# Four places in place of two for the copied gate and up columns of the experts, each copied one block sooner

## The chip, the cores and the metric

The kernel runs on one core of a Trainium2 chip. The metric is the device time of one execution in microseconds (us), lower is better; what is compared is the median of several runs. The profile is one further execution, recorded by the hardware profiler, and has a time of its own.

## The reference, cut to what matters

The input x has 4 sequences of 1024 tokens with 256 channels. It is normalised, and two things are added to it: a windowed self-attention, and a mixture of experts with one shared expert and 64 routed ones, of which each token uses eight. The change touches the routed experts alone:

```python
gate_out = jnp.einsum('bsh,ehi->bsei', hidden_states, expert_gate_k)
up_out = jnp.einsum('bsh,ehi->bsei', hidden_states, expert_up_k)
expert_act = jax.nn.silu(gate_out) * up_out
routed = jnp.einsum('bsei,eih->bsh', expert_act * router_mask[..., None], expert_down_k)
```

All of it is float32. An expert's weights are a 256 x 128 gate, a 256 x 128 up and a 128 x 256 down matrix.

## The kernel before

The program runs five stages one after the other: `project` (normalisation, q, k, v, router), `route` (sorting the 32768 pairs of token and expert into 320 blocks of 128 slots, one expert to a block; also the shared expert), `experts`, `attend` and `merge`. Semaphores are set and awaited by hand. The change is in `experts` alone, about 270 to 883 us of the profile.

**A block** (r) goes through this chain. GpSimd gathers its 128 token rows from DRAM into one of 16 places of `xb` (L903), once the result of block r-16 has been taken. TensorE transposes them into PSUM (L923, `turn_x`), ScalarE copies that to `xTe` (L970, `copy_x`), and TensorE forms gate and up, in this order, from `xTe` and the weights in `wgu` (L934, `gate_up`). ScalarE applies silu to the gate (L978), VectorE multiplies by up (L1021), TensorE multiplies by the down matrix (L944, `down`), VectorE scales the result by the token's weight into one of four places of `ys` (L1030, `take_y`), and SyncE stores it (L869). A place of `ys` is written again when the store of four blocks before has landed.

**Weights.** An expert's three matrices come by one DMA into one of eight places of `wb`. SyncE issues it in step r for block r+8, behind the store of block r (L479); it moves bytes only where block r+8 is the first of its expert. ScalarE copies the 512 gate and up columns from `wb` to `wgu` (L986, `copy_w`) for every block; the down matrix is read from `wb` directly.

**Order of the work.** All engines run their own instructions in the order written. A loop turn has 16 blocks; the first and last turn stand outside the loop, 18 are in it. In step r TensorE does `down(r)`, `turn_x(r+3)`, `gate_up(r+2)`; ScalarE does `copy_x(r+3)`, `silu(r+2)`, `copy_w(r+3)`; VectorE does the product of r+1, then `take_y(r)`; SyncE stores r and issues the weights of r+8. `wgu` has NW = 2 places, so `copy_w(r)` waits until the up product of block r-2 is done, besides the landing of its weights. `gate_up(r)` waits for `wgu_ready`, for `xTe` and for the product of block r-2, whose PSUM banks it takes over. The last four loop turns (blocks 256 to 319) also load the first stacks of q and k for `attend`, one DMA at every fourth block.

Of the kernel before, what the change touches and what calls it, by code (L numbers as in the profile page):

```python
# [67 lines left out]
WCOLS = 2 * 2 * I + D  # L68
XR = 16
WR = 8  # L70
# [413 lines left out]
def fields(engine, table, n, at, most):  # L484


    regs = [engine.alloc_register(f"entry_{next(NUMBER)}") for k in range(n)]
    engine.load(regs, table[0:1, bass.ds(at, n)])
    return [bass.RuntimeValue.of_register_unchecked(reg, min_val=0, max_val=most) for reg in regs]


def unpack(words, k, most):


    word = words[k // PACK]
    return ((word >> (PACK_BITS * (k % PACK))) & ((1 << PACK_BITS) - 1)).with_bounds(min_val=0, max_val=most)
# [310 lines left out]
def experts(nc, ctx, keep, w_exp):  # L807
# [9 lines left out]
    def sb(name, shape, dt=F32):  # L817
        return ctx.enter_context(nc.sbuf_tensor(name, shape, dt))
# [4 lines left out]
    def sems(name, n):  # L823
        return [sem(f"{name}{i}") for i in range(n)]

    NW = 2

# [5 lines left out]
    aT = sb("aT", [P, 2, P])  # L835
    wgu = sb("wgu", [P, NW, 2, 2 * I])

# [12 lines left out]
    def first(i):  # L850
        return isinstance(i, int) and i == 0

    def exists(i, r):
        return not isinstance(i, int) or i * XR + r < NB_ROUTED

    def every(engine, step):

        step(0)
        with engine.Fori(1, LAST) as i:
            step(i)  # L860
        step(LAST)

    with nc.Block() as block:
        @block.sync
        def _(sp):
            def store(i, r):

                sp.wait_ge(ys_ready, i * XR + r + 1)
                sp.dma_start(y_d[bass.ds(i * (XR * P) + r * P, P), :], ys[:, r % YR, :]).then_inc(y_out[r % YR], 16)  # L869

            def step(i, stacks=None):


                for r in range(XR):
                    if stacks is not None and r % 4 == 2:
                        load_stack(sp, keep, stacks[0], stacks[0], stacks[1], r // 4)
                    if r % 8 == 0:
                        load = fields(sp, meta[:, LOAD_F, :], 8, i * XR + (r + WR), (WR << PLACE_BIT) - 1)
                    store(i, r)
                    if exists(i, r + WR):  # L880
                        sp.wait_ge(y_ready, i * XR + (r + 1))
                        load_weights(sp, keep, w_exp, r, load[r % 8])

            step(0)
            with sp.Fori(1, LAST - 3) as i:
                step(i)
            for k in range(4):
                step(LAST - 3 + k, (k // 2, k % 2))
# [27 lines left out]
        def _(pe):  # L916
# [10 lines left out]
            def gate_up(i, r):  # L927
# [4 lines left out]
                for part, bank, ready in ((0, G, g_ready), (1, U, u_ready)):  # L932
                    for h in range(2):
                        last = nc.tensor.matmul(banks[bank + r % 2][:, 0:P],  # L934
                                                wgu[:, r % NW, h, part * I:(part + 1) * I], xT[:, r % 2, h, :],
                                                start=(h == 0), stop=(h == 1))
# [26 lines left out]
        @block.scalar  # L963
        def _(act):
            def copy_x(i, r):

                if not first(i) or r > 1:
                    act.wait_ge(u_ready, i * XR + (r - 1))
                act.wait_ge(px_ready, i * XR + r + 1)
                nc.scalar.copy(xT[:, r % 2, :, :].rearrange("p h q -> p (h q)"), banks[PX + r % 2][:, 0:D]  # L970
                               ).then_inc(xT_ready, 1)

            def silu(i, r):

                if not first(i) or r > 1:
                    act.wait_ge(act_ready, i * XR + (r - 1))
                act.wait_ge(g_ready, i * XR + r + 1)
                nc.scalar.activation(gate[:, r % 2, :], banks[G + r % 2][:, 0:P], ACT.Silu).then_inc(gate_ready, 1)  # L978

            def copy_w(i, r, at):  # L980


                act.wait_ge(w_in[r % WR], i * (16 * XR // WR) + 16 * (r // WR + 1))
                if not first(i) or r >= NW:
                    act.wait_ge(u_ready, i * XR + (r - NW + 1))
                nc.scalar.copy(wgu[:, r % NW, :, :].rearrange("p h c -> p (h c)"), wb[:, bass.ds(at, 4 * I)]  # L986
                        ).then_inc(wgu_ready, 1)

            def step(i):
                words = fields(act, packed[:, AT_F, :], XR // PACK + 1, i * (XR // PACK), WORD)  # L990
                at = [unpack(words, k, WR - 1) * WCOLS for k in range(XR + 3)]
                for r in range(XR):
                    if exists(i, r + 3):
                        copy_x(i, r + 3)
                    if exists(i, r + 2):
                        silu(i, r + 2)
                    if exists(i, r + 3):
                        copy_w(i, r + 3, at[r + 3])

            words = fields(act, packed[:, AT_F, :], 1, 0, WORD)  # L1000
            at = [unpack(words, k, WR - 1) * WCOLS for k in range(3)]
            copy_w(0, 0, at[0])
            copy_w(0, 1, at[1])
            copy_x(0, 0)
            copy_x(0, 1)
            silu(0, 0)
            copy_w(0, 2, at[2])
            copy_x(0, 2)
            silu(0, 1)
            every(act, step)  # L1010

        @block.vector
# [593 lines left out]
def build(nc, x, w_qk, w_vr, w_proj, w_exp, c_f32, out):  # L1606
    with ExitStack() as ctx:
# [44 lines left out]
        with ExitStack() as inner:  # L1652
            experts(nc, inner, keep, w_exp)
# [56 lines left out]
```

## Time and profile before

| | |
|---|---|
| median of 3 runs | 1404.14 us (1404.03 to 1408.12) |
| the profiled execution's own time | 1411.81 us |
| its span in the trace | 1410.0 us |
| granted TensorE clock, mean over the span | 0.946 of full speed |
| busy, share of the span | TensorE 88%, weight loads of TensorE 58%, VectorE 58%, ScalarE 56%, GpSimd 46% |

In rows of the profile PE is TensorE's matmuls, PEld its loads of the stationary operand, DVE VectorE, ACT ScalarE, POOL GpSimd, and SPq the DMA instructions of SyncE. A float32 matmul stands there as two instructions. A bracket at the end of a row gives how long the engine was idle before it and what ended that; "issue" is time in which it waited for nothing that the profile shows.

### The profile page before, as it was taken

How to read it: one execution, taken by the hardware profiler on the slowest of the kernel's cores; microseconds unless marked ns; L12 is line 12 of the kernel's file. 1: busy time of each engine (PE TensorE's matmuls, PEld its weight loads, DVE VectorE, ACT ScalarE, POOL GpSimd, SP SyncE). 2: the span in 40 equal slices, each digit the busy share in tenths (PEclk: the TensorE clock that was granted, in tenths of full speed). 3: DMA queues.
4: the chain of work that ended last, by engine and by line, in shares of the span. 5: the costliest groups of instructions: out<-in, count | busy, mean ns of one | idle time of the engine just before them, and what ended most of it. 6: DMA issues, size and time to landing. Idle time of an engine off the chain costs nothing. (4 is left out here: it accounts for less than half of the span.)

```text
span 1410.0 us, 37368 instructions
## 1 busy us (share of the span) xinstructions
PE 1241.7 (88%) x8360; PEld 824.5 (58%) x8361; DVE 824.4 (58%) x2576; ACT 785.9 (56%) x1900; POOL 644.4 (46%) x666
## 2 busy tenths in 40 slices
PE   6777699679999999998999889888888888888879
PEld 3444366568888788887888768233334333344337
DVE  5778588524444344443444334878777777777733
ACT  3444345446777677775777656255555554555553
POOL 1333303255555455554555443555555555555520
PEclk9999899889999999999999999799989999889989
DMA  7677600167777677775777897255544545444413
GB/s 249 182 185 189 171 1 23 41 170 209 213 215 211 195 218 213 210 220 177 217 210 230 199 163 145 76 131 126 143 116 116 129 125 130 124 114 116 119 46 120
DMA packets 150486, 218.01 MB, mean 155 GB/s; under 512 B 22817, under 2 KB 123169, under 8 KB 150434
## 3 DMA queue, kind: packets, MB, share of 16 engines
q1 hardware_dynamic: 121954, 130.59, 31.7%
q0 software_dynamic: 27648, 86.02, 25.1%
q10 hardware_dynamic: 832, 0.79, 0.2%
q8 instruction: 23, 0.38, 0.1%
q14 instruction: 29, 0.24, 0.1%
HBM read 247.46 MB, written 70.26 MB: 225 GB/s over the span
## 5 line engine op out<-in xcount | busy, mean ns | idle before, releaser
L903 POOL DMA_INDIRECT xb<-token_rows,idx_ring_x x320 | 304.0, 950 | 280.3 <-issue 180.3
L934 PE MATMUL psum<-xTe,wgu 128*128 128x128 f32 x2560 | 372.8, 289 | 23.4 <-ACT wgu L986 22.2
L934 PEld LDWEIGHTS psum<-xTe,wgu 128*128 128x128 f32 x2560 | 314.5, 193 | 82.2 <-ACT wgu L986 60.3
L1521 POOL DMA_INDIRECT yg<-expert_rows,idx_ring x256 | 260.4, 1017 | 209.9 <-PE psum L1229 130.0
L1351 ACT ACTIVATE pT<-psum 128x384 f32<-128x384 f32 (+1 forms) x512 | 218.3, 465 | 227.8 <-PE psum L1229 198.0
L1416 DVE CUSTOM_DVE_ANT_0 masked<-psum,mask_q 128x384 f32<-128x384 f32 (+1 forms) x512 | 252.9, 520 | 89.4 <-PE psum L1236 48.5
L1030 DVE TENSOR_SCALAR ys<-psum,xb 128x256 f32<-128x256 f32 x320 | 154.9, 484 | 155.8 <-PE psum L944 113.6
L1021 DVE TENSOR_TENSOR aT<-gate,psum 128x128 f32<-128x128 f32 x320 | 91.9, 287 | 213.6 <-PE psum L934 169.6
L1236 PE MATMUL psum<-qk 96*128 96x384 bf16 (+1 forms) x512 | 176.5, 347 | 40.9 <-DVE nmax L1416 32.4
L986 ACT COPY wgu<-wb 128x512 f32 x320 | 198.5, 620 | 12.3 <-PEq L544 4.4
L944 PE MATMUL psum<-wb,aT 128*128 x640 | 195.6, 388 | 9.7 <-DVE aT L1021 6.8
L1244 PE MATMUL psum<-qk 98*128 98x384 bf16 (+1 forms) x512 | 173.9, 341 | 12.7 <-ACT pT L1351 10.6
L970 ACT COPY xTe<-psum 128x256 f32<-128x256 f32 x320 | 119.4, 373 | 82.8 <-PE psum L923 32.9
L978 ACT ACTIVATE gate<-psum 128x128 f32<-128x128 f32 x320 | 89.0, 278 | 119.5 <-issue 77.3
L1229 PE MATMUL psum<-consts_bf 128*128 128x256 bf16 (+1 forms) x512 | 142.5, 279 | 0.0
L1257 PE MATMUL psum<-pT,va 128*32 128x256 f32 (+1 forms) x1792 | 129.7, 363 | 0.2 <-ACT pT L1351 0.2
L923 PE MATMUL psum<-ident,xb 128*128 128x128 f32 x640 | 123.8, 276 | 6.7 <-DMA xb<-token_rows,idx_ring_x 6.7
L1236 PEld LDWEIGHTS psum<-qk 96*128 96x128 bf16 x512 | 53.3, 104 | 105.1 <-DVE nmax L1416 58.6
L923 PEld LDWEIGHTS psum<-ident,xb 128*128 128x128 f32 x640 | 90.8, 142 | 40.0 <-DMA xb<-token_rows,idx_ring_x 7.5
L944 PEld LDWEIGHTS psum<-wb,aT 128*128 128x128 f32 x640 | 98.1, 194 | 14.4 <-issue 14.1
L1244 PEld LDWEIGHTS psum<-qk 98*128 98x128 bf16 x512 | 51.8, 101 | 92.8 <-issue 44.3
L1454 DVE TENSOR_TENSOR yg<-yg 128x512 f32<-128x512 f32 (+1 forms) x128 | 79.7, 624 | 0.1
(139 smaller groups left out, 1175.2 us busy)
## 6 DMA issues: line engine op xcount, KB each, us to landing
wb<-in_w_exp SPq DMA_DIRECT2D x320, 384.0 KB
expert_rows<-ys SPq DMA_DIRECT2D x320, 128.0 KB
qk<-q_stacks SPq DMA_DIRECT2D x32, 384.0 KB
q_stacks<-wb SPq DMA_DIRECT2D x32, 192.0 KB, 2.7
qk<-k_parts SPq DMA_DIRECT2D x32, 192.0 KB
k_parts<-wb SPq DMA_DIRECT2D x28, 192.0 KB, 2.7
token_rows<-rows SPq DMA_DIRECT2D x8, 640.0 KB, 3.3
xb<-token_rows,idx_ring_x POOLq DMA_INDIRECT x320
```

The costliest lines, as they stand in the source:

```text
L903: nc.gpsimd.indirect_dma_start(out=xb[:, r, :], out_offset=None, in_=rows_d, in_offset=bass.IndirectOffsetOnAxis(ap=idx_ring[:, q, r:r + 1 ...
L923: last = nc.tensor.transpose(banks[PX + r % 2][:, h * P:(h + 1) * P], xb[:, r % XR, h * P:(h + 1) * P], ident[:, :])
L934: last = nc.tensor.matmul(banks[bank + r % 2][:, 0:P], wgu[:, r % NW, h, part * I:(part + 1) * I], xT[:, r % 2, h, :], start=(h == 0), sto ...
L944: nc.tensor.matmul(banks[Y + r % 2][:, 0:D], aT[:, r % 2, :], wb[:, bass.ds(at + 4 * I, D)], start=True, stop=True).then_inc(y_ready, 1)
L986: nc.scalar.copy(wgu[:, r % NW, :, :].rearrange("p h c -> p (h c)"), wb[:, bass.ds(at, 4 * I)]).then_inc(wgu_ready, 1)
L1030: nc.vector.tensor_scalar(ys[:, r % YR, :], banks[Y + r % 2][:, 0:D], xb[:, r % XR, bass.ds(e + W_COL, 1)], None, ALU.mult).then_inc(ys_re ...
L1229: return nc.tensor.matmul(out, ident_b, mask, start=False, stop=True, skip_group_check=True)
L1236: nc.tensor.matmul(ring_bank(ahead_entry(like(g), i, hh))[:, 0:(hi - lo) * P], qk[0:KS, q, 0, hh, i * P:(i + 1) * P], qk[0:KS, q, 1, hh, l ...
L1244: nc.tensor.matmul(key_bank(j, hh)[:, 0:(hi - lo) * P], qk[0:KM, q, 1, hh, j * P:(j + 1) * P], qk[0:KM, q, 0, hh, lo * P:hi * P], start=Tr ...
L1351: nc.scalar.activation(pT[:, (j % 2) * HG + hh, 0:(hi - lo) * P], key_bank(j, hh)[:, 0:(hi - lo) * P], ACT.Exp).then_inc(p_ready, 1)
L1416: nc.vector.tensor_tensor_reduce(masked[:, (i * HG + hh) % 2, 0:(hi - lo) * P], ring_bank(place)[:, 0:(hi - lo) * P], mask_q[:, side:side ...
L1521: nc.gpsimd.indirect_dma_start(out=yg[:, h, k, :], out_offset=None, in_=y_d, in_offset=bass.IndirectOffsetOnAxis(ap=idx_ring[:, h, k:k + 1 ...
```

## The change

`wgu` gets four places, and ScalarE copies the columns of block r+4 in step r, where it copied those of block r+3. The copy of a fourth block is added ahead of the first turn. Each copy then waits for the up product of block r-4 in place of r-2. The number of copies is the same, and TensorE's order is the same.

```diff
-    NW = 2
+    NW = 4
...
-                at = [unpack(words, k, WR - 1) * WCOLS for k in range(XR + 3)]
+                at = [unpack(words, k, WR - 1) * WCOLS for k in range(XR + NW)]
                 for r in range(XR):
                     if exists(i, r + 3):
                         copy_x(i, r + 3)
                     if exists(i, r + 2):
                         silu(i, r + 2)
-                    if exists(i, r + 3):
-                        copy_w(i, r + 3, at[r + 3])
+                    if exists(i, r + NW):
+                        copy_w(i, r + NW, at[r + NW])
...
-            at = [unpack(words, k, WR - 1) * WCOLS for k in range(3)]
+            at = [unpack(words, k, WR - 1) * WCOLS for k in range(NW)]
...
             silu(0, 1)
+            copy_w(0, 3, at[3])
             every(act, step)
```

## Rows read from the trace of the kernel before

**Rows 1.** The page: engines over the span, and the groups of lines 934 and 986.
```profile
PE 1241.7 (88%) x8360; PEld 824.5 (58%) x8361; DVE 824.4 (58%) x2576; ACT 785.9 (56%) x1900; POOL 644.4 (46%) x666
L934 PEld LDWEIGHTS psum<-xTe,wgu 128*128 128x128 f32 x2560 | 314.5, 193 | 82.2 <-ACT wgu L986 60.3
L986 ACT COPY wgu<-wb 128x512 f32 x320 | 198.5, 620 | 12.3 <-PEq L544 4.4
```

**Rows 2.** Windows: length, PE, PEld, DVE, ACT, POOL busy, PE clock, DMA share, GB/s.
```profile
322.00:761.00 439.00, 428.22 (x2885) 356.15 (x2886) 185.61 (x482) 302.56 (x722) 231.44 (x257) 1.00 0.71 210
761.00:799.00 38.00, 34.91 (x237) 28.95 (x236) 14.79 (x40) 24.51 (x60) 18.51 (x22) 1.00 0.75 207
799.00:865.00 66.00, 58.81 (x396) 48.90 (x395) 23.85 (x65) 40.42 (x100) 34.47 (x31) 1.00 1.01 175
```

**Rows 3.** Timeline of one block's step: start, duration, engine, line, operation.
```profile
503.02 0.97 PEld L934 LDWEIGHTS psum<-xTe,wgu 128*128 128x128 f32 x8 [0.21 <-ACT wgu L986]
...
503.21 0.48 DVE L1030 TENSOR_SCALAR ys<-psum,xb 128x256 f32<-128x256 f32 x1 [0.42 <-PE psum L944]
503.83 0.28 ACT L978 ACTIVATE gate<-psum 128x128 f32<-128x128 f32 x1 [0.37 <-issue]
504.13 0.62 ACT L986 COPY wgu<-wb 128x512 f32 x1
504.28 0.29 DVE L1021 TENSOR_TENSOR aT<-gate,psum 128x128 f32<-128x128 f32 x1 [0.58 <-PE psum L934]
504.80 0.97 PEld L934 LDWEIGHTS psum<-xTe,wgu 128*128 128x128 f32 x8 [0.20 <-ACT wgu L986]
504.87 0.37 ACT L970 COPY xTe<-psum 128x256 f32<-128x256 f32 x1
505.61 0.28 ACT L978 ACTIVATE gate<-psum 128x128 f32<-128x128 f32 x1 [0.36 <-issue]
```

**Rows 4.** Timeline of the weight loads of TensorE across the end of a loop turn.
```profile
524.37 0.97 PEld L934 LDWEIGHTS psum<-xTe,wgu 128*128 128x128 f32 x8 [0.20 <-ACT wgu L986]
525.67 0.30 PEld L944 LDWEIGHTS psum<-wb,aT 128*128 128x128 f32 x2 [0.33 <-issue]
525.99 0.36 PEld L923 LDWEIGHTS psum<-ident,xb 128*128 128x128 f32 x2
526.32 0.97 PEld L934 LDWEIGHTS psum<-xTe,wgu 128*128 128x128 f32 x8
527.21 0.30 PEld L944 LDWEIGHTS psum<-wb,aT 128*128 128x128 f32 x2
```

**Rows 5.** Timeline: the results of blocks 16, 256, 276, 308 and 319 being taken.
```profile
322.18 0.48 DVE L1030 TENSOR_SCALAR ys<-psum,xb 128x256 f32<-128x256 f32 x1
760.66 0.48 DVE L1030 TENSOR_SCALAR ys<-psum,xb 128x256 f32<-128x256 f32 x1 [0.68 <-PE psum L944]
799.25 0.48 DVE L1030 TENSOR_SCALAR ys<-psum,xb 128x256 f32<-128x256 f32 x1 [0.35 <-PE psum L944]
865.00 0.48 DVE L1030 TENSOR_SCALAR ys<-psum,xb 128x256 f32<-128x256 f32 x1 [0.85 <-DMA expert_rows<-ys]
882.47 0.48 DVE L1030 TENSOR_SCALAR ys<-psum,xb 128x256 f32<-128x256 f32 x1 [0.61 <-PE psum L944]
```

**Rows 6.** Timeline of SyncE's DMA instructions and the gathers between them.
```profile
504.22 0.35 SPq L869 DMA_DIRECT2D expert_rows<-ys  x1
504.50 0.95 POOL L903 DMA_INDIRECT xb<-token_rows,idx_ring_x  x1 [0.77 <-issue]
505.14 0.67 SPq L479 DMA_DIRECT2D wb<-in_w_exp  x1
505.91 0.35 SPq L869 DMA_DIRECT2D expert_rows<-ys  x1
```

**Rows 7.** Timeline and windows: one load that moves bytes, and the traffic after it.
```profile
508.63 0.30 SPq L479 DMA_DIRECT2D wb<-in_w_exp  x1
510.00:512.00 2.00, 1.96 (x15) 1.48 (x13) 0.77 (x2) 1.37 (x5) 1.17 (x2) 1.00 0.94 311
```

## The prediction, made before the changed kernel was run

> **What bounds the kernel now.** I read the page first. TensorE is the busiest engine, and what held up its gate and up weight loads longest is one instruction of ScalarE, the copy that the change moves: 60.3 of 82.2 us of idle time [rows 1]. The windows then say where: from block 16 to 256 the TensorE clock is full throughout, DMA is at 0.71 and nothing else is near its limit, and this stretch, 439 us, is where a turn repeats itself; behind it come two stretches with the q and k stacks in the way, the second with DMA at 1.01 [rows 2].
>
> The timeline of one step shows the ring that sets the pace. Gate and up of a block start at 503.02. Silu starts at 503.83, as soon as the gate is done. The copy of the next block's columns is queued behind silu and runs 504.13 to 504.75. The next gate and up start 0.05 later, at 504.80, after 0.20 of idle time put down to that copy [rows 3]. So the ring is 0.81 (gate product and signal) + 0.30 (silu) + 0.62 (copy) + 0.05 = 1.78 us, and 504.80 - 503.02 is 1.78. The copy has nothing to do with the silu ahead of it; only ScalarE's order puts it there, and with a look-ahead of one block it is due at once.
>
> Over a whole stretch: from the taking of block 16 to that of block 256 it is 760.66 - 322.18 = 438.48 us, 1.827 a block, two stalls of a few us included [rows 5].
>
> **The change, part by part.**
>
> *The copy one block sooner, into a ring of four.* TensorE then finds its columns ready: they were finished a block earlier, and the copy's own wait (up product of r-4, done before the silu in front of it can start) ends long before. What TensorE needs by itself can be read where ScalarE was not late, at the end of a loop turn: down's loads 525.67, the transposes' 525.99, gate and up 526.32, down again 527.21. That is 0.32 + 0.33 + 0.89 = 1.54 us [rows 4]. It is the floor of the new step: 0.24 less than 1.78.
>
> *What is late next.* ScalarE: copy of the columns to start of the xTe copy 504.13 to 504.87 = 0.74, xTe copy to silu at most 0.74 as it stands with its wait of 0.36, so 0.38 without it, silu to copy 0.30: 1.42 a block, under 1.54 [rows 3]. With gate and up starting at t, silu is at t+0.81, the copy ends at t+1.73, the xTe copy runs t+1.85 to t+2.22, and the next silu is due at t+1.54+0.81 = t+2.35. xTe is needed at t+3.08. VectorE's product ends at 504.57, 1.55 after its gate and up began; down needs it at 1.54+0.89 = 2.43 [rows 3, 4]. These covers hold. Were ScalarE to take over, its 1.42 would still be below TensorE.
>
> *Ends of the loop turn.* From 524.37 to 526.32 is 1.95, of which 1.54 is work; TensorE's own loop end costs 0.41 [rows 4]. It is now partly hidden in ScalarE's ring and comes out in full: 15 times between block 16 and 256, 6 us.
>
> *The added copy ahead of the first turn, one more place number per turn to unpack, 4 KB a partition.* One copy is 0.62 [rows 1] while no block can be computed; bounds 0 and +0.6, I take 0. The unpacking is a few register instructions that ScalarE runs ahead in its spare time: 0. The last step of the last turn has one copy fewer: 0.
>
> *Weights are wanted one step sooner.* `copy_w` is queued ahead of the next xTe copy and silu, so a late DMA would stop all three and through them TensorE. SyncE issues the load behind the store; for the block whose result is taken until 503.69 that is 505.14, 1.45 later; allow 1 to 2 [rows 3, 6]. In a step the column copy starts 0.44 after that end, at 504.13 [rows 3]. The copy now comes four steps later, 4 x 1.54 + 0.4 = 6.6 us after that result, so 4.6 to 5.6 us are left for the DMA; with five steps of 1.78 it was 7.3 and more. The one load that I followed was issued at 508.63 and its burst of 311 GB/s is over by about 512, some 3.4 us [rows 7]. Cost 0, upper bound below.
>
> *SyncE and GpSimd, whose steps must shrink as well.* Stores go out 1.69 us apart (504.22, 505.91), which is near the block's time; but the load's instruction at 505.14 took 0.67 and ended just after the gather 504.50 to 505.45, so SyncE seems to be held by each gather's end and keeps step with it, rather than being full [rows 6]. GpSimd is 0.95 busy in a step and then waits for block r-16 [rows 6]. Value: no cost. The other bound, SyncE unable to go below 1.69, is a rival.
>
> **The sum**, by the taking of results [rows 5]:
> - blocks 3 to 16, same step: 13 x 0.24 = 3.
> - blocks 16 to 256: 240 x 1.54 + 15 x 0.41 + stalls. Stalls now: 438.48 - 240 x 1.78 = 11.3, of which 15 x 0.17 are what the loop ends (1.95 - 1.78) show; 8.7 stay. New 369.6 + 6.2 + 8.7 = 384.5; gain 54.
> - blocks 256 to 276, 38.59 us, DMA at 0.75: between 0 and 20 x 0.24 = 4.8; I take 3.
> - blocks 276 to 308, 65.75 us with DMA at 1.01 [rows 2] and VectorE waiting for stores of four blocks before: that is not TensorE's time; 0 to 3, I take 0.
> - blocks 308 to 319: 11 x 0.24 = 2.6; 2.
> Together 62. The floor 1.54 rests on one loop end and supposes no wait of any kind, so I take 1.56 for the 284 blocks in this sum: 6 less, 56. Made against the profiled execution, whose own time is 1411.81 for a span of 1410.0, that gives 1356; it is 7.7 above the median of the runs shown. Against the median: 1404.14 - 56 = 1348. The stages behind shift and keep their length.
>
> *A rule against the trace.* Matmul rows are busy 428 of 439 us in the main stretch, and the weight loads 356 [rows 2]. By the first row TensorE is full and 11 us are all there is to win; but the start-to-start times say that 0.20 and more of each step is idle, and they carry the sum. The Trainium skill (Perfetto Trace Analysis, Identifying the Most-Contended Engine) holds matmul busy time to be a bad measure of what is left, and weight-load busy time a better one. By that rule, 83 us would be open here, the overlap of loads not counted; the trace agrees with its direction, and the sum uses neither figure.
>
> **The rivals.**
> 1. *SyncE is the next bound.* For: stores 1.69 apart although nothing on TensorE asks for just that [rows 6]. Against: the load's 0.67 looks like being held, and 0.92 from store to load + 0.1 would leave room. Then the step is 1.69: 0.09 x 240 + 5 = 27 us, 1377.
> 2. *DMA latency grows* as the same bytes move in 0.87 of the time: share 0.71 x 1.78/1.56 = 0.81, and stores or gathers land late in the bursts. Step 1.65: 0.13 x 240 + 4 = 35, 1369.
> 3. *No change*: TensorE is full as its matmul row says, or the copy's new place does not free it (something unseen on ScalarE makes gate and up wait as before). 1404, at best 1395.
> 4. *Slower: the copy waits for its weights.* Place: `copy_w` of the first block of each new expert, some 56 of them, once DMA takes longer from issue to landing than the 4.6 to 5.6 us left. It decides from there: each further us costs 1 us x 56, with xTe copy and silu stuck behind. To end above 1404 + 4 the loads have to come 1.1 us too late on average, 6 us or more against 3.4 seen [rows 7]; at 1.2 us, 1348 + 67 = 1415.
>
> **How the numbers follow.** Forecast 0.69 (1338 to 1360), SyncE 0.14, DMA 0.08, no change 0.05, slower 0.04. A measurement of this kernel tells 0.3%, 4 us, from nothing. Faster by more: 0.69 + 0.14 + 0.08 = 0.91; within: 0.05; slower: 0.04. The time is that of the forecast, 1348. The range goes from 1338 (the floor of 1.54, and all of the gain of the two middle stretches) to 1378, which takes in rivals 1 and 2 and leaves out some of the forecast's edge and the last two.
>
> **What the changed profile would show.** The idle time before gate and up put down to the copy (60.3 us) nearly gone; weight loads of gate and up 1.54 to 1.57 apart; busy share of ScalarE per us up from 0.69 to 0.78 in the main stretch; block 16 to 256 in 384 to 392 us; the stretch with DMA at 1.01 as long as before. Wrong if SyncE's stores stand 1.69 apart with DVE waiting for landed stores, if ScalarE is idle before the column copies, or if the clock is no longer full.

## The result, and the profile after

The changed kernel takes **1450.64 us** (median of 4 runs, 1449.92 to 1456.79); the kernel before, measured beside it, takes 1404.09 (4 runs, 1403.72 to 1408.12). The ratio is 1.033, with a 95% interval of 1.031 to 1.035: **slower by 46 us**, where 56 us less were forecast. The profiled execution took 1451.01 us for a span of 1449.2.

The page of the changed kernel: the engines, and the groups that answer to [rows 1], with three that grew.

```profile
PE 1194.3 (82%) x8360; PEld 822.2 (57%) x8361; DVE 817.2 (56%) x2576; ACT 761.3 (53%) x1900; POOL 642.8 (44%) x666
...
L934 PEld LDWEIGHTS psum<-xTe,wgu 128*128 128x128 f32 x2560 | 317.6, 195 | 27.7 <-issue 18.1
...
L1022 DVE TENSOR_TENSOR aT<-gate,psum 128x128 f32<-128x128 f32 x320 | 91.4, 285 | 255.9 <-remote 95.1
L986 ACT COPY wgu<-wb 128x512 f32 x320 | 197.8, 618 | 34.5 <-DMA wb<-in_w_exp 21.9
...
L944 PEld LDWEIGHTS psum<-wb,aT 128*128 128x128 f32 x640 | 98.1, 193 | 113.0 <-issue 112.5
```

The change did what it says. The 60.3 us that gate and up waited for the copy are gone from L934, which is now idle for 27.7 in place of 82.2. But every busy share is lower than before, and idle time stands in a new place: 113 us ahead of the down matrix's loads, and 256 us ahead of VectorE's product, 95 of them put down to "remote", where the profile names no instruction of this core as the releaser.

Windows of the changed kernel: block 16 to 256, block 256 to 319, and the two stages behind; columns as in [rows 2].

```profile
320.00:808.00 488.00, 400.78 (x2889) 358.14 (x2887) 179.58 (x481) 282.10 (x722) 231.38 (x257) 0.99 0.64 189
808.00:927.00 119.00, 100.75 (x734) 90.13 (x734) 46.83 (x126) 71.29 (x182) 52.77 (x51) 1.00 0.82 181
927.00:1449.00 522.00, 446.84 (x3680) 215.54 (x3680) 373.86 (x1380) 266.42 (x737) 260.29 (x258) 0.92 0.45 116
```

The loss sits in one stretch. Block 16 to 256 takes 488 us where 384.5 were forecast and 439 were measured [rows 2], with the same work in it (weight loads 358 against 356), a full clock and a lower DMA share than before. Between the two profiled spans (1410.0 and 1449.2) the 39.2 us come about as -2.2 up to block 16, +49.4 from block 16 to 256, -3.1 to block 319, and -4.9 behind, in stages that the change leaves alone.

Timeline of the changed kernel: results of blocks 16, 256 and 319 being taken (to compare with [rows 5]), and between them a stall, and a step without one.

```profile
320.02 0.48 DVE L1031 TENSOR_SCALAR ys<-psum,xb 128x256 f32<-128x256 f32 x1 [0.15 <-issue]
...
390.54 0.97 PEld L934 LDWEIGHTS psum<-xTe,wgu 128*128 128x128 f32 x8
...
390.71 0.94 POOL L903 DMA_INDIRECT xb<-token_rows,idx_ring_x  x1 [0.54 <-issue]
...
391.98 0.38 PE L923 MATMUL psum<-ident,xb 128*128 128x128 f32 x2
392.02 0.02 SPq L869 DMA_DIRECT2D expert_rows<-ys  x1
392.08 0.97 PEld L934 LDWEIGHTS psum<-xTe,wgu 128*128 128x128 f32 x8
...
392.24 0.28 ACT L978 ACTIVATE gate<-psum 128x128 f32<-128x128 f32 x1 [0.51 <-PE psum L934]
392.26 0.94 POOL L903 DMA_INDIRECT xb<-token_rows,idx_ring_x  x1 [0.60 <-issue]
...
392.84 0.00 SPq L479 DMA_DIRECT2D wb<-in_w_exp  x1
393.58 0.00 SPq L869 DMA_DIRECT2D expert_rows<-ys  x1
393.69 0.29 DVE L1022 TENSOR_TENSOR aT<-gate,psum 128x128 f32<-128x128 f32 x1 [2.24 <-remote]
393.72 0.37 ACT L970 COPY xTe<-psum 128x256 f32<-128x256 f32 x1 [0.57 <-PE psum L923]
...
394.42 0.30 PEld L944 LDWEIGHTS psum<-wb,aT 128*128 128x128 f32 x2 [1.36 <-issue]
...
503.49 0.97 PEld L934 LDWEIGHTS psum<-xTe,wgu 128*128 128x128 f32 x8
...
505.03 0.97 PEld L934 LDWEIGHTS psum<-xTe,wgu 128*128 128x128 f32 x8
...
807.88 0.48 DVE L1031 TENSOR_SCALAR ys<-psum,xb 128x256 f32<-128x256 f32 x1
...
926.54 0.48 DVE L1031 TENSOR_SCALAR ys<-psum,xb 128x256 f32<-128x256 f32 x1 [0.61 <-PE psum L944]
```

Where nothing disturbs, the step is 505.03 - 503.49 = 1.54 us, the floor that was forecast. But of the 240 steps between blocks 16 and 256, 75 are longer than 2.3 us (5 in the kernel before). In the stall shown, the product needs silu and the up matmul. The silu ended at 392.52; the matmuls that began at 390.65 are modelled to end at 391.70; the product starts at 393.69. The transposes end at 392.36, and ScalarE, which has been free since 393.15, copies them at 393.72. The trace also records when each semaphore rose. Set beside the modelled end of the matmul that raises it:

```
signal of TensorE        due      seen     late
gate, first block       391.26   392.15   0.89
up, first block         391.70   393.61   1.91
down                    392.14   393.65   1.51
transposes              392.36   393.69   1.33
gate, second block      392.80   393.75   0.95
up, second block        393.25   393.81   0.56
gathers of GpSimd: 390.71 to 391.65 and 392.26 to 393.20
```

TensorE has done the work, but its signals are seen up to 1.9 us later, five of them in a bunch of 0.2 us that begins 0.4 after a gather has ended. SyncE is held as well: one of its register instructions takes from 392.35 to 392.83, and between 392.92 and 393.55 it starts none. ScalarE's signals are not: silu ends at 392.51, inside the second gather, and its signal is recorded at 392.52.

The same shows over the whole stretch from block 16 to 256. Of 770 records of TensorE's semaphores, 372 come more than 0.3 us after the end of the matmul that raises them; of 867 records of the semaphores that ScalarE and VectorE raise, the latest comes 0.012 us after. The starts of the waiting instructions say it without these records: 79 of 720 starts of silu, product and `xTe` copy come over 1 us after the modelled end of all that they need, their own engine being free (3 in the kernel before). Of the 75 long steps, 58 have such a start in them or in the 1.5 us ahead of them.

The waits of the changed kernel between 322 and 800 us (total, times, longest) say the same in sums:

```profile
PEld psum L944 <- issue: 83.2, 68, 3.1
...
DVE aT L1022 <- remote: 64.0, 26, 4.0
ACT xTe L970 <- PE psum L923: 61.7, 87, 3.6
...
ACT wgu L986 <- DMA wb<-in_w_exp: 18.0, 9, 4.2
...
PEld psum L934 <- ACT wgu L986: 7.7, 5, 2.3
```

### The profile page after: what moved, and what is told of

It reads as the page before. It is cut to its first block and busy times, and to the rows that moved or that the text cites. A ratio compares the mean times of both kernels' runs of the same rounds, so it can differ in the third digit from the quotient of the medians.

```text
span 1449.2 us, 37366 instructions
## 1 busy us (share of the span) xinstructions
PE 1194.3 (82%) x8360; PEld 822.2 (57%) x8361; DVE 817.2 (56%) x2576; ACT 761.3 (53%) x1900; POOL 642.8 (44%) x666
## 5 line engine op out<-in xcount | busy, mean ns | idle before, releaser
L934 PE MATMUL psum<-xTe,wgu 128*128 128x128 f32 x2560 | 346.7, 279 | 21.7 <-issue 13.3
L1522 POOL DMA_INDIRECT yg<-expert_rows,idx_ring x256 | 259.6, 1014 | 205.6 <-PE psum L1230 120.2
L934 PEld LDWEIGHTS psum<-xTe,wgu 128*128 128x128 f32 x2560 | 317.6, 195 | 27.7 <-issue 18.1
L944 PE MATMUL psum<-wb,aT 128*128 x640 | 203.6, 400 | 95.7 <-DVE aT L1022 82.6
L986 ACT COPY wgu<-wb 128x512 f32 x320 | 197.8, 618 | 34.5 <-DMA wb<-in_w_exp 21.9
L1237 PE MATMUL psum<-qk 96*128 96x384 bf16 (+1 forms) x512 | 173.4, 342 | 37.0 <-DVE nmax L1417 30.1
```

What stands on the lines that cost most here:

```text
L934: last = nc.tensor.matmul(banks[bank + r % 2][:, 0:P], wgu[:, r % NW, h, part * I:(part + 1) * I], xT[:, r % 2, h, :], start=(h == 0), sto ...
L944: nc.tensor.matmul(banks[Y + r % 2][:, 0:D], aT[:, r % 2, :], wb[:, bass.ds(at + 4 * I, D)], start=True, stop=True).then_inc(y_ready, 1)
L1237: nc.tensor.matmul(ring_bank(ahead_entry(like(g), i, hh))[:, 0:(hi - lo) * P], qk[0:KS, q, 0, hh, i * P:(i + 1) * P], qk[0:KS, q, 1, hh, l ...
L1522: nc.gpsimd.indirect_dma_start(out=yg[:, h, k, :], out_offset=None, in_=y_d, in_offset=bass.IndirectOffsetOnAxis(ap=idx_ring[:, h, k:k + 1 ...
```

## The experiments

The theory after these readings, **G**: while GpSimd issues a gather, TensorE's completion signals and SyncE's instructions are held, and a step of 1.54 leaves too little time between gathers for them. (The first expectation below counts the landings of DMAs among what is held; no run shows that.) The rivals: **W**, the copies wait for their weights, now wanted sooner; **S**, SyncE has too much to issue; **T**, the traffic of the same bytes in less time. The runs came in four sets, each on one chip with the kernel before beside it. One thing has to be known to read them: in the first two sets the kernel before took 1298 to 1299 us; in the last two, on other chips, it took 1419 to 1420, near the 1404 of the first measurement. So times are compared within a set only. The first measurement belongs to none of the sets. That the conditions differ was not known when the expectations of the first set were written.

Of the stretches, this table is worked out from the timelines of all profiles: block 16 to 256 and 256 to 319 by the taking of results, `attend`, how many of SyncE's register instructions between blocks 16 and 256 took over 0.3 us (its loads of table words apart), and of the 240 steps there how many took over 2.3 us, with their median. The last column gives the records of TensorE's four semaphores in the same stretch: how many come over 0.3 us after the last modelled end of a matmul that raises them, of how many there are. All there would be 960, give or take one at an edge; records that are missing are not counted as late.

```
run                          16-256  256-319  attend  SyncE>0.3  steps>2.3  median  TensorE late
before (first measurement)    438.5   121.8   485.1      87          5       1.78  12 of 651
changed (first measurement)   487.9   118.7   480.1     158         75       1.58 372 of 770
-- before = 1298 to 1299 us
e6 before again               429.8   117.4   398.8       0          0       1.78   0 of 954
e1 four places only           428.2   117.1   398.9       0          0       1.78   0 of 955
e2 paced by copy              429.8   117.0   398.5       0          0       1.78   0 of 957
e3 paced by product           404.0   115.9   399.7       0          0       1.66   0 of 949
e5 changed again              372.5   116.5   398.1       0          0       1.55   0 of 852
e4 no gathers                 371.1    96.8   398.5       0          0       1.55   0 of 961
e7 no weight loads            371.1   109.7   398.4       0          0       1.55   0 of 898
e8 plain loads                457.8   115.2   398.8       0         55       1.63   0 of 960
-- before = 1419 to 1420 us
e9 changed, third time        493.8   122.3   487.1     150         78       1.62 329 of 741
e12 paced by product          443.8   121.5   487.3     140         22       1.71  84 of 599
e11 half the gathers          376.8    97.8   488.3      58          8       1.55   3 of 765
e16 no gathers                371.1    96.8   489.5       0          0       1.55   0 of 961
e15 no weight loads           479.3   120.7   488.0       3         75       1.55 389 of 843
e14 plain loads               459.9   115.5   492.4       0         53       1.64   0 of 959
e10 before, no gathers        429.0   111.3   487.5       0          0       1.78   0 of 960
e13 before, plain loads       458.4   116.5   488.6       0         52       1.73   0 of 960
```

### First set: the parts of the change, and its pace

**Four places alone**, the copy where it was:

```diff
-    NW = 2
+    NW = 4
```

> Four places, but the columns copied as late as before. Theory G (the step got too short: while GpSimd issues a gather, the signals of TensorE, of landing DMAs and SyncE's own instructions are held for most of 1.3 us, and a step of 1.54 us leaves too little open time, so that every third step stalls by 1.6 us): the step is 1.78 again, the time that of the kernel before, 1404 within 4. Rival A (the ring of four itself, its addresses or the freed wait, stalls TensorE): 1450.

1296.07 us against 1298.02: 0.998 (0.997 to 0.999). The places are neutral; ScalarE's order alone sets 1.78.

**The change, but gate and up held back** until one more copy is done, so that the early copies stay and the pace does not:

```diff
-                pe.wait_ge(wgu_ready, i * XR + r + 1)
+                pe.wait_ge(wgu_ready, i * XR + r + (2 if exists(i, r + 1) else 1))
```

> The changed kernel, with gate and up of block r waiting for the column copy of block r+1 as well: it puts ScalarE's copy back in the ring and the step back to 1.78, while every copy still comes one block sooner. Theory G: 1404 within 6, the stalls of 1.6 us gone. Rival W (copies wait for late weights, which stops silu and the xTe copy behind them): stays near 1450, since the weights are wanted as early as in the changed kernel; at 1.78 a step W would give some of it back, 1430 or so.

1298.27: 1.0005 (0.999 to 1.002). Early copying by itself costs and brings nothing. Neither of these two was run again where the kernel before takes 1404 or more.

**The change, with gate and up waiting for the product of block r-1** in place of r-2, a pace in between:

```diff
-                    pe.wait_ge(act_ready, i * XR + (r - 1))
+                    pe.wait_ge(act_ready, i * XR + r)
```

> The changed kernel, with gate and up of block r waiting for the product of block r-1 in place of r-2: a step of about 1.60 to 1.62. Theory G: the open time per step goes from some 0.2 to 0.3 us; either the stalls become rarer (time between 1360 and 1440), or they stay at every third to fourth step (1440 to 1470). Rival A and W: 1445 to 1470, the longer step on top of the same stalls.

1269.16: 0.978 (0.976 to 0.980), step 1.66 and no stall. The expectation missed, for the reason that the next set shows.

**The change without gathers** after the first 16 blocks:

```diff
-                    nc.gpsimd.indirect_dma_start(
+                    if first(i) and q == 0:
+                        nc.gpsimd.indirect_dma_start(
...
-                pe.wait_ge(x_in[r % XR], i * 16 + 16 * (r // XR + 1))
+                if first(i) and r < XR:
+                    pe.wait_ge(x_in[r % XR], 16)
```

> The changed kernel without the gathers of blocks 16 to 319: the rows of the first 16 blocks stay in xb and are used again; all else, the waits of GpSimd too, stays. Theory G: TensorE's signals come at once, the step is 1.54 without stalls, block 16 to 256 in 375 to 385 us, and with the slow stretch at the end gone too the time is 1320 to 1345. Rivals S (SyncE's stores and loads are the bound) and W: stalls stay, block 16 to 256 over 450 us.

1213.98 in one run, a step of 1.55. By itself this tells nothing on the stalls, since the kernel before stood at 1298 here and the changed kernel had not been run beside it.

### Second set: the changed kernel elsewhere

> The changed kernel once more, unaltered, beside the kernel before. In the runs of the last four kernels the kernel before took 1298 in place of 1404, so the two comparisons may not be made under the same conditions. Theory H (the stalls of the changed kernel belong to the conditions of the first measurement, under which the chip holds signals for longer): where the kernel before takes 1298, the changed one has a step of 1.54 without stalls and takes 1235 to 1260; where it takes 1404, 1450. Theory G as it stood (a step of 1.54 is always too short for the gathers): the ratio is 1.03 here too.

> The kernel before once more, for its trace under the conditions of this call. If they are those of the last one: step 1.78, block 16 to 256 in 428 us, no 12.97 us stop at the first block, attend about 85 us shorter than in the first trace. If they are those of the first trace: 1404.

The changed kernel takes **1234.38 us against 1298.93: 0.951 (0.949 to 0.954)**, faster by 64.5. The kernel before, as a run of its own, took 1296.68. Windows of the changed kernel in this set, block 16 to 256 and 256 to 319:

```profile
302.00:674.00 372.00, 371.74 (x2880) 346.93 (x2879) 184.75 (x480) 296.51 (x720) 234.03 (x260) 1.00 0.84 249
674.00:791.00 117.00, 103.14 (x743) 93.25 (x741) 46.61 (x127) 75.20 (x183) 53.83 (x53) 0.96 0.83 187
```

Its groups in the stretch of the first window:

```profile
L934 PEld LDWEIGHTS psum<-xTe,wgu 128*128 128x128 f32 x1919 | 233.2, 192 | 0.4 <-issue 0.4
...
L986 ACT COPY wgu<-wb 128x512 f32 x240 | 148.5, 619 | 16.3 <-DMA wb<-in_w_exp 10.4 <-PE psum L934 1.0 <-issue 0.3
```

Same instructions, 372 us in place of 488, and the DMA engines carry 249 GB/s where the first measurement had 189. So the traffic of this pace is no bound (against T), and SyncE issues everything 1.54 apart (against S). G as it first stood, for every chip, falls as well: from here on it is a theory of the conditions under which the kernel before takes 1404 or more. What differs is in the kernel before as well. Timeline of SyncE and GpSimd in it, as e6, where [rows 6] shows a load instruction of 0.67 us that ends with the gather:

```profile
502.60 0.94 POOL L903 DMA_INDIRECT xb<-token_rows,idx_ring_x  x1 [1.02 <-DVE ys L1030]
...
502.89 0.09 SPq L479 DMA_DIRECT2D wb<-in_w_exp  x1
...
503.63 0.35 SPq L869 DMA_DIRECT2D expert_rows<-ys  x1
```

Here it takes 0.09 beside the gather. None of some 2200 register instructions of SyncE in the stretch takes over 0.09 us; in the first measurement of the same kernel 87 took over 0.3, up to 0.72. The semaphore records agree: in e6 all 954 come within 0.02 us of the modelled end, in the first measurement 12 of 651 are late. A missing record is not a late one: for 4 of 240 transposes e6 has no record within 0.3 us and the first measurement none for 105, but e5, in which nothing stalls, has none for 74.

**No weight loads** (copies and products use the eight first ones), and **plain loads**, where SyncE fetches the same bytes and the gathers are left out as in e4:

```diff
-                    if exists(i, r + WR):
-                        sp.wait_ge(y_ready, i * XR + (r + 1))
-                        load_weights(sp, keep, w_exp, r, load[r % 8])
```
```diff
+                    if exists(i, r + XR):
+                        sp.dma_start(xb[:, r, :], rows_d[r * P:(r + 1) * P, :]).then_inc(x_more[r], 16)
```

> The changed kernel without any weight DMA in experts: the eight places of wb hold the first eight experts throughout, SyncE stores only, and the copies wait for no DMA. Theory W or S: where the changed kernel stalls, this one does not, step 1.54 throughout. Theory G or H: where the changed kernel stalls, this one stalls as well, within 15 us of it in block 16 to 256.

> The changed kernel with the gathers of blocks 16 to 319 replaced by plain DMAs of the same 128 x 1280 bytes, issued by SyncE behind each store: the same bytes move, but GpSimd builds no descriptors, and the rows are not the right ones. Theory G: no stalls, since what hurts is GpSimd's issuing. If the DMA traffic itself holds the signals: stalls as in the changed kernel. SyncE has one DMA more per block, some 0.4 to 0.5 us; it may become the bound at 1.6 to 1.9.

Without weight loads it took 1225.07, 9 less. With plain loads it took 1322.41, and this is a loss of another kind, the same in both conditions (457.8 and 459.9 us, below): stores land late. It bounds what a plain load can tell, but not whether SyncE is held.

### Third set: pace and gathers where the change loses

> The changed kernel a third time. Under the conditions of the first measurement (kernel before near 1404): 1450. Under those of the two calls since (kernel before near 1298): 1234. The other kernels of this call are read by which of the two it is.

> The kernel before without the gathers of blocks 16 to 319. Where the kernel before takes 1298: step 1.78 still, 428 us for block 16 to 256, and the slow last 64 blocks at 1.78 too, in all some 10 us less, 1285 to 1290. Where it takes 1404, theory G (GpSimd's gathers hold up signals of TensorE and SyncE under those conditions): its stalls of 3 to 13 us in experts vanish, SyncE's register instructions are never held for 0.3 us or more between block 16 and 256, and it ends near 1370, attend being as it was.

> The changed kernel without the gathers of the blocks with an odd number from block 17 on. Where the kernel before takes 1298: step 1.54, and a slow end of half the length, 1220 to 1228. Where it takes 1404, theory G: the gathers leave half of the time open, stalls go, 1310 to 1350; a theory in which the short step alone stalls TensorE: 1440 to 1450.

> Gate and up of block r waiting for the product of r-1, a step of 1.66, once more. Where the kernel before takes 1298: 1269 again. Where it takes 1404, theory G: between the kernel before and the changed one or better than both, 1380 to 1440, depending on whether 0.1 us more of open time per step is enough.

The kernel before took 1420.14 (9 runs). The changed kernel lost again: 1471.82 (2 runs; 1450 had been expected), 1.037 (1.027 to 1.048), with 78 long steps. The edit of e11 leaves out the gathers of odd blocks behind the first 16, and only those: 1326.04 in one run, **146 us less than with all of them**, 8 long steps. Of the 146 us, 117 lie in block 16 to 256 and 25 in block 256 to 319. Windows of e11, block 16 to 256:

```profile
320.00:697.00 377.00, 374.31 (x2886) 348.17 (x2885) 184.89 (x481) 295.16 (x721) 116.94 (x136) 1.00 0.64 191
```

The middle pace, e12, took 1416.38: 0.998 (0.994 to 1.001), with 22 long steps. So with all gathers in place a step of 1.78, 1.66 and 1.54 has 5, 22 and 78 long ones, the 5 from the first measurement. The kernel before without gathers took 1391.09, no register instruction of SyncE held; it was expected near 1370, but its stretch from 16 to 256 was nearly without stalls already (438.5 in the first measurement, 429.0 here).

### Fourth set: gathers, bytes and weights apart

> The kernel before with the gathers of blocks 16 to 319 replaced by plain DMAs of the same bytes issued by SyncE, one more DMA per block for SyncE. Where the kernel before takes over 1400: if GpSimd's issuing does the holding, no register instruction of SyncE between block 16 and 256 takes 0.3 us or more, and none of the stops of 3 us; if the traffic does it, they are there as with gathers. Step 1.78 to 1.9.

> The changed kernel with plain loads once more (1322 where the kernel before took 1298, VectorE waiting for late stores). Where the kernel before takes over 1400: if GpSimd's issuing is the cause, experts takes as long as it did in the other conditions, the rest of the program its longer time, 1410 to 1425 in all; if traffic is, more than 1440.

> The changed kernel without weight DMAs. Where the kernel before takes over 1400: theory G, stalls of 1.6 us at every second to fourth step as in the changed kernel, block 16 to 256 over 460 us and the whole over 1420; rivals W and S: step 1.54, block 16 to 256 under 385 us. Elsewhere 1225 again.

> The changed kernel without the gathers of blocks 16 to 319. Where the kernel before takes over 1400: step 1.54 without stalls, block 16 to 256 in 372 us, in all about 1320, some 6 below the one with half of the gathers. Elsewhere 1214 again.

The kernel before took 1418.97 in one run; each kernel below was run once, and the changed kernel itself not at all in this set. **Without gathers** the changed kernel took 1322.02, with no long step. The first window is block 16 to 256, the second the two stages behind, whose gathers were left as they are:

```profile
320.00:691.00 371.00, 371.00 (x2882) 346.92 (x2882) 185.19 (x481) 299.94 (x720) 2.97 (x15) 1.00 0.45 142
788.00:1320.00 532.00, 455.96 (x3680) 218.81 (x3680) 375.19 (x1380) 266.95 (x737) 259.04 (x258) 0.91 0.44 114
```

371 us is what e5 needed with all gathers, and what e4 needed. `attend`, with 256 gathers of its own (L1522), stays at 489.5.

**Without weight loads** it took 1450.49. Waits of e15 in block 16 to 256:

```profile
DVE aT L1018 <- remote: 97.8, 41, 3.0
PEld psum L939 <- issue: 90.2, 72, 2.4
...
ACT xTe L965 <- PE psum L918: 75.2, 138, 3.8
```

There are 75 long steps, as many as the changed kernel had, with no weights to wait for and a third of SyncE's register instructions left (734 of 2200): **W and S fall**. Only 3 of those instructions are held, and yet 389 of 843 signals of TensorE are late. So the count of held instructions of SyncE does not tell whether TensorE's signals are held; the last column does.

**With plain loads** both kernels are above 1418.97 (1427.39 and 1432.14), the changed one a little more than expected, and e13 has 52 long steps where none was expected. Window and waits of e14 in block 16 to 256:

```profile
320.00:780.00 460.00, 395.77 (x2881) 358.35 (x2880) 181.17 (x481) 279.35 (x721) 2.95 (x15) 0.98 0.67 199
...
DVE ys L1038 <- DMA expert_rows<-ys: 155.2, 104, 3.3
ACT wgu L993 <- DMA wb<-in_w_exp: 121.6, 50, 3.7
```

These are waits for landings, of a DMA queue given 160 KB more at each step, and e8 has the first of them too (151.7 us, 105 times). But none of 959 signals of TensorE is late, no register instruction of SyncE takes over 0.3 us, and the stretch takes the same time in both conditions. The traffic is no smaller than in the changed kernel (199 GB/s against 189), though its average step is longer than 1.54. What differs between the conditions goes with the gathers that GpSimd issues and not with their bytes: **T falls, G stands**.

## Why the prediction was wrong

**The forecast failed in its step "SyncE and GpSimd ... Value: no cost"**, and with it in "What is late next ... These covers hold". The row at 505.14 [rows 6] was read rightly, as SyncE held by the gather, and then priced as if only SyncE's spare time were at stake. The covers were worked out with signals that take no time. Product and down had 2.43 - 1.55 = 0.88 us of slack by that step; the stall above shows the up signal 1.91 late, and block 16 to 256 took 487.9 us where the sum had 384.5. Nothing in the quoted rows says that TensorE's signals are held too. The trace of before had signs of it outside the rows: a first step of 13.0 us, whose product is the second line here,

```profile
280.87 0.48 DVE L1030 TENSOR_SCALAR ys<-psum,xb 128x256 f32<-128x256 f32 x1 [1.31 <-PE psum L944]
293.53 0.29 DVE L1021 TENSOR_TENSOR aT<-gate,psum 128x128 f32<-128x128 f32 x1 [12.17 <-remote]
```

and which takes 1.6 us in e6, and the 8.7 us of "stalls of a few us" that the sum carried along as a constant. The prediction counted two stalls; there are five steps over 2.3 us, four of them with an instruction that starts over 0.5 us after TensorE had done its part. They were no constant: a shorter step makes many of them.

**The rest of the sum was right**, as the profile of e5 against that of e6 shows (span 1294.9 to 1229.9, 65.0 less; forecast 62 before the 6 that were taken off):
- *The ring of 1.78 and the floor of 1.54.* The step is 1.55, and idle time put down to the copy falls from 52.7 us over the whole of e6 to 1.8 in e5. In block 16 to 256: 429.8 to 372.5, a gain of 57.3 for the term of 54. The 6 us taken off for a step of 1.56 were not there.
- *End of a loop turn*, 0.41 exposed: too much. The 15 turns took 24.83 on the mean, and 16 x 1.54 is 24.64, so 0.19.
- *Blocks up to 16*, term 3: 3.3, with the stage's earlier start of 1.0 taken off. *Blocks 256 to 319*, terms 3 + 0 + 2: only 1.0 came, so hardly any of this stretch is TensorE's time. Without gathers it takes 96.8 (e4).
- *Weights one step sooner*, cost 0: the copies wait 15.8 us for weights in e5 and 21.9 in the first measurement; before, all of their idle time was 12.3 [rows 1]. That is not nothing, but leaving out the loads gains only 1.4 us from block 16 to 256 (e5 to e7), and it ends no stall (e15).
- *The added copy, the unpacking, four places*, cost 0: e1 and e2 bear that out to 0.2%.

**The rivals.** SyncE as a bound at 1.69: no, it keeps 1.54 where it isn't held, though it was the engine that showed the holding. DMA latency: no (e5 at 249 GB/s). No change: matmul rows were full in e5 as well, 371.74 of 372 us, while the stretch had become 57 us shorter. The rival on the slower side named the wrong wait: its result, 1415 by late weights, was not reached by weights. A rival "signals are held during gathers" was not among them.

*The rule against the trace.* Matmul rows were full at a step of 1.78 (428 of 439) and at 1.54, so they told nothing of what could be won. The weight loads were busy 356 of 439 us [rows 2], and 347 of 372 in e5. The Trainium skill (Perfetto Trace Analysis, Identifying the Most-Contended Engine) has it so; e5 used 57 of the 83 us that its measure left open, and in the first measurement none.

## What is shown, and what stays open

Shown: the loss needs the gathers (e16, e11), it needs the pace (e12, e9), it needs neither weight loads (e15) nor the bytes of the gathers (e14), and it is absent in the other condition (e5). That held signals of TensorE are the link is read from the last column of the table: they are late by the hundred in the three runs with 75 to 78 long steps (changed, e9, e15), in 84 records where there are 22 (e12), and in none where no gathers are issued. A part of the records is missing, so these counts are no exact shares.

Not shown is why a step of 1.78 escapes. That its signals fall between two gathers is not the reason, or not alone: in the kernel before, 231 of 240 transposes end while a gather runs, and only 4 of their copies start over 0.5 us late. In the changed kernel 185 of 240 gate products end while a gather runs; all 38 silus that start over 0.5 us late are among these, but the other 147 are prompt. So for the gate a running gather is needed and does not suffice, and no run moved a gather within its step. Open too: why some chips hold signals and others do not. The chip couldn't be chosen and each was used in one set, so the chip and the moment are not told apart. A plain load differs from a gather in its issuer, its queue and its addressing at once, and no plain load was issued by GpSimd, so these three are not told apart either. Nor was it tried whether the kernel's place in memory or the recording of the profile plays a part.

No version beat both kernels in both conditions. The changed kernel is the best where nothing is held (0.951), and loses 3 to 4% where signals are. The version paced by the product (e3, e12) gives 0.978 and 0.998, and was in neither condition slower than the kernel before.

## What to carry to other kernels

A cover worked out from one step's rows holds only with signals as prompt as in that step. Before shortening a step, look through the whole stretch for steps that are longer than the rest, for waits put down to "remote", and for register or DMA instructions that take 0.7 us beside a neighbour's 0.09, and set the records of a semaphore beside the ends of the instructions that raise it. Such rows price a resource that the regular step doesn't show, and their number can grow with the pace. Where a kernel issues a gather in each step, time a faster step at more than one pace, and on more than one chip, before believing either sign.

## What the runs showed of the hardware that was not expected

- The same program took 1298 to 1299 us on two chips, and 1404 to 1420 in the first measurement and on two others. The difference lies in stages with gathers: `attend` 399 against 485 (480 to 492 over all kernels under the second condition), the first step of the experts 1.6 against 13.0; the first gather of the experts starts at 268.3 in e6 and 269.5 in the first measurement, and `merge` takes 41 in both. For `attend` that is where the difference lies and not its cause: no run left out its gathers, and the granted clock over `attend` and `merge` differs too (0.97 in e1 and 0.98 in e5, against 0.91 and 0.92 in the first measurement and 0.91 in e16).
- Beside a gather of 0.95 us, in the second of these conditions, SyncE's register instructions take up to 0.73 us in place of at most 0.09, and TensorE's signals are seen 0.6 to 1.9 us late in the stall shown, while those of ScalarE and VectorE are never more than 0.02 us late. In the changed kernel the gather itself takes 0.947 us in both, the product 0.285 and 0.287. The Trainium skill (SBUF — State Buffer, SBUF: two separate sides) knows one contention on the engines' side of the SBUF, an exclusive lock on the ports that GpSimd shares with VectorE. Those two durations are where a wait for it would be looked for, and they are equal; so no row here supports it as the cause.
- Leaving out the gathers of the last blocks, whose empty slots by the kernel's code all fetch one and the same row, takes block 256 to 319 from 116.5 to 96.8 us (e5, e4), 20 us, where the 240 blocks before gain 1.4.
